# Attention and ternary FFN block on one core: the product of latents and probabilities in tiles of 64 rows by 32 columns, two blocks of V at a time

## What is computed

```python
Q = (h @ Wq.T + bq)                 # 16 heads of 32
V = (h @ Wv.T + bv)
attn_logits = einsum('bhtd,lhd->bhtl', Q, latent) / sqrt(32)   # 64 latents per head
topk_logits, topk_idx = top_k(attn_logits, 4)
weighted = einsum('bhtk,bhtkd->bhtd', softmax(topk_logits), selected latents)
attn_output = (weighted + V) @ Wo.T + bo
x = x + layernorm(attn(layernorm(x)))
hidden = silu(x' @ wu.T) * (x' @ wg.T)          # wu, wg, wd ternary
x = x + layernorm(hidden @ wd.T)
```

## Time and profile before

| | |
|---|---|
| median of 3 runs | 1194.86 us (1194.04 to 1199.66) |
| span of the profiled execution | 1194.9 us |
| TensorE (PE) matmuls busy | 1046.1 us, 88% of the span |
| VectorE (DVE) busy | 782.7 us, 65% |
| ScalarE (ACT) busy | 520.5 us, 44% |
| GpSimd (POOL) busy | 456.7 us, 38% |
| one `mid` chunk | some 133 us, six of them |

### The profile page before, as it was taken

The page is one execution under the profiler, slowest core; times in us unless marked ns, Lnnn a source line. Parts: engine busy times, 40 slices in busy tenths (PEclk is TensorE's granted clock), DMA queues, the critical chain, the costliest instruction groups (busy, mean ns, idle before and its releaser), DMA issues. The chain is left out here.

```text
span 1194.9 us, 16632 instructions
## 1 busy us (share of the span) xinstructions
PE 1046.1 (88%) x5044; PEld 487.4 (41%) x5044; DVE 782.7 (65%) x2781; ACT 520.5 (44%) x793; POOL 456.7 (38%) x374
## 2 busy tenths in 40 slices
PE   2623598999899998999899989999899999998997
PEld 1322243444444443444444444444444444443443
DVE  6499775975488375965498476965498467936433
ACT  4577454533445424534445434434444443532330
POOL 1138132552256232643256233633256233632230
PEclk9856698999899998999899998999899999999999
DMA  7831321123301231123301321123202320121000
GB/s 223 323 105 36 71 54 53 36 41 84 88 18 35 72 78 44 35 53 74 85 18 35 85 65 44 36 53 81 79 18 41 85 68 1 36 53 39 15 1 36
DMA packets 152448, 74.60 MB, mean 62 GB/s; under 512 B 136768, under 2 KB 136768, under 8 KB 151360
## 3 DMA queue, kind: packets, MB, share of 16 engines
q1 hardware_dynamic: 152384, 73.95, 24.8%
HBM read 31.99 MB, written 8.39 MB: 34 GB/s over the span
## 5 line engine op out<-in xcount | busy, mean ns | idle before, releaser
L573 PE MATMUL ug<-X1T,TU 128*128 128x512 f16 x1024 | 251.3, 390 | 19.9 <-DVE ugt L1194 15.6
L573 PE MATMUL ug<-X1T,TG 128*128 128x512 f16 x1024 | 241.9, 379 | 0.0
L977 POOL TENSOR_TENSOR hT<-ugt,hT 128x512 f16<-128x512 f32 x128 | 148.0, 1156 | 220.8 <-ACT hT L815 219.8
L583 PE MATMUL ring<-TD,hT 128*128 128x512 f16 x1024 | 224.5, 379 | 0.0
L808 ACT ACTIVATE ugt<-ug,cu 128x512 f32<-128x512 f32 x128 | 87.8, 686 | 185.1 <-PE ug L573 184.2
L573 PEld LDWEIGHTS ug<-X1T,TU 128*128 128x128 f16 x1024 | 100.6, 100 | 150.0 <-DVE ugt L1194 28.3
L1189 DVE SCALAR_TENSOR_TENSOR ugt<-ugt,ug 128x512 f32<-128x512 f32 x128 | 87.0, 680 | 98.6 <-ACT ugt L808 98.6
L573 PEld LDWEIGHTS ug<-X1T,TG 128*128 128x128 f16 x1024 | 100.2, 98 | 121.0 <-issue 0.4
L583 PEld LDWEIGHTS ring<-TD,hT 128*128 128x128 f16 x1024 | 99.6, 98 | 122.0 <-ACT p L797 2.5
L964 POOL TENSOR_TENSOR Lb<-Lb,v 128x1024 f32<-128x1024 f32 x32 | 82.3, 2571 | 66.4 <-DVE Lr L1226 59.2
L1226 DVE MATCH_REPLACE8 Lr<-v,Lb 128x68 f32<-128x68 f32 x512 | 102.3, 212 | 0.0
(11 more groups left out here) (170 smaller groups left out, 1562.9 us busy)
## 6 DMA issues: line engine op xcount, KB each, us to landing
x_in<-in_L_attn_hidden_states SPq DMA_DIRECT2D x8, 1024.0 KB, 4.9
out_dram<-Lr SPq DMA_DIRECT2D x32, 256.0 KB, 3.3
x<-in_L_attn_hidden_states SPq DMA_DIRECT2D x28, 256.0 KB, 3.5
hT<-in_L_ffn_W_up SPq DMA_DIRECT2D x8, 512.0 KB, 7.8
hT<-in_L_ffn_W_down SPq DMA_DIRECT2D x8, 512.0 KB, 4.1
TD<-in_L_ffn_W_gate SPq DMA_DIRECT2D x4, 512.0 KB, 11.2
TU<-in_L_attn_Wq SPq DMA_DIRECT2D x1, 1024.0 KB, 7.8
TG<-in_L_attn_Wv SPq DMA_DIRECT2D x1, 1024.0 KB, 9.2
```

The source lines that it names most:

```text
L573: last = pe.matmul(ug[:, 2 * (e % 2) + s, :], w[:, k, e * P:(e + 1) * P], X1T[:, b, k, :], start=(k == 0 and b == 0), stop=(k == KD - 1 an ...
L583: last = pe.matmul(ring[:, bank, :], hT[:, a, e, t * P:(t + 1) * P], td[:, e, :], start=(e == 0 and a == 0), stop=(e == NE - 1 and a == 1))
L977: pool.tensor_tensor(hT[:, 1, e, :], ugt[:, 2 + e % 2, :], hT[:, 0, e, :], ALU.subtract).then_inc(h_lo, 1)
```

## The change

`latV` loses its zeros: it holds 32 columns per block, the latents of one head on partitions 0 to 63 and those of another on 64 to 127. The heads are put in another order in `Lb` (and so in `PT`), so that block 4a + r holds head r of V block 2a in its upper half and head r of V block 2a + 1 in its lower half. `vw(a)` now makes two blocks of V. It takes both banks first, does both projections (24 matmuls), and then three products of eight matmuls, each on a tile of 64 rows by 32 columns, rows 0 to 63 into the one bank and rows 64 to 127 into the other. TensorE runs `vw(0)`, `vw(1)` in place of the four blocks; in the `first` body these stand after `ternary(17)` and `ternary(21)`. The orders of ScalarE, VectorE, GpSimd and SyncE stay, but for two memsets that go.

```diff
-        latV = [sb(f"latV_{s}", [P, H // 2, 2 * HD], F16) for s in ("hi", "lo")]
+        latV = [sb(f"latV_{s}", [P, H // 2, HD], F16) for s in ("hi", "lo")]
...
+        own_wait_pe = sem("own_wait_pe")
...
-                def vw(m):
-                    bank = bank_of("VW", 0, m)
-                    if m == 0 and kind == "first":
+                def vw(a):
+
+                    banks = [bank_of("VW", 0, 2 * a + s) for s in range(2)]
+                    if a == 0 and kind == "first":
                         pe.wait_ge(wt_lo, 3 * KD)
-                    project(1, bank, m, False)
-                    if m == 0:
-                        wait(pe, p_t, i, 16 * TT, 16 * TT)
+                    for s in range(2):
+                        project(1, banks[s], 2 * a + s, False)
+                    if a == 0:
                         if kind == "first":
                             pe.wait_ge(lat_lo, 2)
-                    for n, (a, c) in enumerate(((0, 0), (0, 1), (1, 0))):
-                        for s in range(2):
-                            last = pe.matmul(ring[64 * s:64 * s + 64, bank, :], latV[a][:, 2 * m + s, :],
-                                             PT[:, c, 2 * m + s, :], start=False, stop=(n == 2), skip_group_check=True)
-                    last.then_inc(vw_done, 1)
+                        wait(pe, p_t, i, 16 * TT, 16 * TT)
+                        pe.sem_inc(own_wait_pe, 1)
+                    for n, (b, c) in enumerate(((0, 0), (0, 1), (1, 0))):
+                        for r in range(4):
+                            for s in range(2):
+                                rows = slice(64 * s, 64 * s + 64)
+                                last = pe.matmul(ring[32 * r:32 * r + 32, banks[s], :], latV[b][rows, 4 * a + r, :],
+                                                 PT[rows, c, 4 * a + r, :], start=False, stop=(n == 2), skip_group_check=True)
+                                if n == 2 and r == 3:
+                                    last.then_inc(vw_done, 1)
...
-                    after = {3: [(weights, 2)], 5: [(logits, 2)], 8: [(logits, 3)], 15: [(vw, 0)],
-                             17: [(vw, 1)], 19: [(vw, 2)], 21: [(vw, 3)],
+                    after = {3: [(weights, 2)], 5: [(logits, 2)], 8: [(logits, 3)], 17: [(vw, 0)], 21: [(vw, 1)],
                              23: [(wo, 0), (wo, 1), (wo, 2), (wo, 3)]}
...
-                    for m in range(KD):
-                        vw(m)
+                    vw(0)
+                    vw(1)
...
-                        act.activation(Lb[:, t % 2, 8 * b:8 * b + 8, 0:NL],
-                                       ring[:, plan[("L", 0, 2 * t + b)][0], :].rearrange("p (h l) -> p h l", h=8),
+                        act.activation(Lb[:, t % 2, 8 * b:8 * b + 8, 0:NL].rearrange("p (r s) l -> p r s l", s=2),
+                                       ring[:, plan[("L", 0, 2 * t + b)][0], :].rearrange("p (s r l) -> p r s l", s=2, r=4),
                                        ACT.Copy, scale=clo[:, 0:1]).then_inc(l_ready, 1)
...
             for s in range(2):
-                pool.memset(latV[s][:, :, :], 0.0)
                 pool.memset(latL[s][:, :, :], 0.0)
```

More of the change, by code:

```diff
@@ L714, in latV_hi @@
                         rows = slice(NL * hh, NL * hh + NL)
-                        last = act.activation(latV[0][rows, :, hh * HD:(hh + 1) * HD],
-                                              latr[rows, :].rearrange("p (j h d) -> p j h d", h=2, d=HD)[:, :, hh, :],
+                        last = act.activation(latV[0][rows, :, :].rearrange("p (a r) d -> p a r d", a=2),
+                                              latr[rows, :].rearrange("p (a h r d) -> p a h r d", a=2, h=2, d=HD)[:, :, hh, :, :],
                                               ACT.Copy, scale=up[rows, 2:3])
@@ L1175, in latV_lo @@
                         rows = slice(NL * hh, NL * hh + NL)
-                        last = dve.scalar_tensor_tensor(out=latV[1][rows, :, hh * HD:(hh + 1) * HD],
-                                                        in0=latr[rows, :].rearrange("p (j h d) -> p j h d", h=2, d=HD)[:, :, hh, :],
-                                                        scalar=up[rows, 2:3], in1=latV[0][rows, :, hh * HD:(hh + 1) * HD],
+                        last = dve.scalar_tensor_tensor(out=latV[1][rows, :, :].rearrange("p (a r) d -> p a r d", a=2),
+                                                        in0=latr[rows, :].rearrange("p (a h r d) -> p a h r d", a=2, h=2, d=HD)[:, :, hh, :, :],
+                                                        scalar=up[rows, 2:3], in1=latV[0][rows, :, :].rearrange("p (a r) d -> p a r d", a=2),
                                                         op0=ALU.mult, op1=ALU.subtract)
```

## The result

The changed kernel takes 1228.96 us (median of 4 runs, 1227.83 to 1229.56) against 1196.2 us for the kernel before in the same comparison: a ratio of 1.0272, 95% interval 1.0257 to 1.0287. It is slower by 2.7%, and the 1227 us of the forecast are 2 us off. Its profiled execution has a span of 1227.8 us, 32.9 us over the 1194.9 us of before.

The account below looks back on a forecast made before the run. TensorE's program order was taken to bound the six mid chunks. From 1194.9 us, +12.5 (wait less gain) +10 (clock) +10 (first body) -0.4 (last body) gave 1227 us, range 1208 to 1242.

Parts of the forecast that it names:

- The bank: In mid chunks TensorE asks too early for the bank VectorE still holds (DN1's): about 3.9 us idle per chunk.
- The rivals with the bank free in time: VectorE frees DN1's bank before TensorE asks: 1184 us (chance 0.04), or 1194 us with the first body's loss (0.04).
- The products: In vw, a step of eight tile matmuls takes 0.22 us; a pair of V blocks gains 0.87 us.
- issue-bound: In the vw products, a step of eight takes 0.44 us, limited by instruction issue: 1234 us, chance 0.06.
- the serial rival: In the vw products, the eight tiles run one after the other, without idle time: about 1260 us, chance 0.06.
- The clock: In mid chunks TensorE runs at half clock after the new idle time: 1.7 us each, 10 us in six.
- wait less gain: In mid chunks the moved bank wait outweighs the products' gain: down(2) starts 2.1 us later, 12.5 us in six.
- The first body: ScalarE's later read-out of vw(0) holds up evictions behind it; wo(0) starts near 169.3 instead of 159.12 us: +10 us.
- The last body: DN1's bank is free early, TensorE gains 1.7 us, but wo waits for two read-outs: net -0.4 us.
- The sum: Over the whole kernel: profiled span 1194.9 us + 12.5 + 10 + 10 - 0.4 = 1227 us, chance 0.80.

Follow-up runs that it names:

- e1: Kernel before, with only TensorE's request for VW3's bank moved ahead of the projection of VW2; old tiles and first body: 1218.78 us, ratio 1.0199.
- e2: Changed kernel, but vw(a) asks for its second bank only between its two projections: 1203.77 us.
- e5: Changed kernel, with VectorE's f_a(1) and f_b(1) put ahead of the two s1_lo so the bank is released earlier: 1193.64 us, ratio 0.9971.
- e6: Changed kernel; second bank requested between projections, VectorE's f_a(1), f_b(1) before s1_lo, first body's vw behind ternary(15) and ternary(19): 1183.03 us, ratio 0.9881.
- e4: Changed kernel, with 16 extra matmuls (3.5 us) per mid chunk filling TensorE's time before the bank wait: 1216.45 us.
- e3: Changed kernel, with the first body's vw(0) and vw(1) on TensorE moved back behind ternary(15) and ternary(19): 1218.33 us.
- e9: Changed kernel, with ScalarE's first-body read-outs of V blocks paired at steps 18 and 22, behind the evictions; TensorE's order unchanged: 1220.69 us.
- e8: Kernel before, with the changed kernel's pairing and first-body places, but the old 128x64 products and old order of heads: 1230.46 us.

## Why the prediction was right, step by step

- **The bank.** Right in place, cause and size: idle time of 3.9 us forecast, 3.85 measured, released by VectorE's `f_b(1)`; e1 has the loss without the tiles, e2 and e5 take it away. The rivals with the bank free in time are out.
- **The products.** Taken at 0.22 us for a step of eight, measured 0.22. The issue-bound and the serial rival are out. The Trainium skill ("TensorE: Matmul & The Clock Gate", Part 2, step 2) gives about 62 ns of sequencer time for a MATMUL where hardware decoding is off, which would be an estimated 0.50 us for the step. This trace does not show it, as the eight matmuls started within 0.22 us. The Trainium skill ("TensorEngine Tiling (Array Packing)", Gotcha 1: PSUM Pressure) also says that different row tiles may not use one PSUM bank at the same time. No run here tries it with one bank; taking two was the step to heed, as its price was the wait.
- **The clock.** Forecast 1.7 us per mid chunk. The chunk grew by 3.54 us; 2.11 of these are wait less gain, namely the wait of 3.85 less the 1.74 that four `vw` take less without a wait (13.84 before, 12.10 in e6). So 1.4 are left, and e4 gives 2.0. The place behind the wait is shown. That the size came close is in part luck: behind five of the six waits the half clock cost 2.4 to 2.9 us, more than behind either idle time from which the prediction took its 1.7 (1.65 and 2.2), behind one it cost nothing, and the 0.6 to 1.2 us that came back at the logits were not in the sum.
- **The first body.** `wo(0)` forecast at 169.3 us, measured 169.53, through the chain that was named; e3 and e9 remove it from both sides. The term was still too small by 2.4 us in the profiled execution: 10 forecast, 12.4 measured, because `wo` itself then ran at half the clock up to 173.3 us (nine matmuls at 0.426 instead of 0.216 us, 1.9 us), which the sum did not have. In e4, whose first body is the same, it was 8.1 us, so this term is known to some 4 us only.
- **The last body.** Forecast -0.4 us, measured -0.3.
- **The sum.** 12.5 + 10 + 10 - 0.4 was forecast; measured 12.7 for wait less gain, 8.1 for the clock in the mid chunks, 12.4 and -0.3: 32.9 us. The first body's surplus and the clock's smaller share cancel, so the total is closer to the forecast than its terms are.

## What to carry to other kernels

Before work on an in-order engine is batched, list the waits that the batch moves to its front, and look up for each how long before its use it is released today: a wait with half a microsecond of room shows nowhere, and here it cost 2% when it moved by 3 us. Look also at what stands behind an unchanged step of another engine that now waits longer (the evictions behind ScalarE's read-out). When a saving turns into idle time, find the release and move that: three edits of order made a slower kernel 1.2% faster than the one it came from.

## What the runs showed of the hardware

Eight matmuls on tiles of 64 rows by 32 columns, the upper four into one bank and the lower four into another, passed 512 columns each in 0.22 us, the time of one full matmul (0.216 us), with 384 of them in the run. Idle TensorE is not neutral: e4 put 3.5 us of useless matmuls into each wait and took 2.0 us less per chunk. But the length of the idle time alone does not tell whether the clock falls: it fell behind five of six waits of 3.85 us (changed kernel), behind four of six of 3.0 us (e1) and behind none of six of 1.1 us (e2). And kernels of different work came to the same chunk length: the changed kernel and e8 both have chunks of 136.5 us in a row (136.55 and 136.58; 136.54, 136.54 and 136.55), though in e8 each chunk has 1.3 us more of products, 0.65 of it behind the wait. In e8 the clock falls for a shorter time behind the wait; the stretch of 14 us around it in a later chunk, e8 first, then the changed kernel:

```profile
692.00:706.00 14.00, 10.79 (x53) 4.29 (x50) 2.95 (x8) 4.79 (x9) 2.97 (x4) 0.88 0.11 38
```

```profile
556.00:570.00 14.00, 10.15 (x77) 3.65 (x76) 2.95 (x8) 4.47 (x8) 2.85 (x3) 0.76 0.12 40
```

The clock of these 14 us is 0.88 against 0.76, and `down(2)` starts 32.16 and 32.24 us after `down(0)`, so what the tiles save behind the wait is lost to the slower clock there. That the two come out so nearly equal was measured and not explained.
